# Row sums once per head pair in four column groups, one product for both heads in narrow slots, and a new spread of the shared bank

## The reference, cut to what matters

```python
q_blhd = jnp.einsum('bld,dhk->blhk', x_bld, Wq)
latent_bll = jnp.einsum('bld,dc->blc', x_bld, Wkv_down)
k_blhd = jnp.einsum('blc,chk->blhk', latent_bll, Wk_up)
v_blhd = jnp.einsum('blc,chk->blhk', latent_bll, Wv_up)
attn = jnp.einsum('bqhd,bkhd->bhqk', q_blhd, k_blhd) / 8
attn = softmax(where(key <= query, attn, -inf))
y_blhd = jnp.einsum('bhqk,bkhd->bqhd', attn, v_blhd)
x = layernorm(x + jnp.einsum('bqhd,hdo->bqo', y_blhd, Wout))
# then: router, top-1 expert with 320 places, gated expert, x + out * gate, layernorm
```

## Time and profile before

| | us |
|---|---|
| median of 3 runs | 2690.92 (2690.39 to 2691.18) |
| the profiled execution | 2683.09 |
| its span | 2681.3 |
| pairs of attention, from the first slot (51.4) to the last one's start (2319.6) | 2268.2 |
| PE busy | 2494.3 |
| POOL busy | 1701.7 |
| DVE busy | 1550.2 |
| ACT busy | 1002.2 |

### The profile page before, as it was taken

One profiled execution on the slowest core, in us unless ns is written; L12 is line 12 of the kernel. 1 busy time (PEld: TensorE's weight loads), 2 busy tenths in 40 slices (PEclk: granted clock), 3 DMA queues, 4 the chain that ended last, 5 costly groups with the idle time before them and its releaser, 6 DMA issues.

```text
span 2681.3 us, 35897 instructions
## 1 busy us (share of the span) xinstructions
PE 2494.3 (93%) x12072; PEld 1588.2 (59%) x12072; DVE 1550.2 (58%) x4378; ACT 1002.2 (37%) x1496; POOL 1701.7 (63%) x1671
## 2 busy tenths in 40 slices
PE   6999999999999999999999999999999999869996
PEld 4555665556655665566556655566556655646663
DVE  4566556665666566655665566656665665235553
ACT  3344334442444334433444244424443344112222
POOL 1677656865687658766786568656876578414444
PEclk7999999999999999999999999999999999879998
DMA  2121100200020001100110002000200011135441
GB/s 81 56 80 56 37 13 13 68 17 13 17 63 18 13 13 41 43 13 17 27 53 17 9 17 67 17 13 17 60 21 13 13 40 43 44 105 161 153 155 57
DMA packets 97062, 118.91 MB, mean 44 GB/s; under 512 B 12480, under 2 KB 75976, under 8 KB 96880
## 3 DMA queue, kind: packets, MB, share of 16 engines
q1 hardware_dynamic: 89712, 99.98, 13.3%
q0 software_dynamic: 7168, 16.64, 1.7%
HBM read 46.91 MB, written 37.90 MB: 32 GB/s over the span
## 4 chain that ended last, share of the span: by engine, by line
PE 63%; POOL 17%; issue 11%; DVE 5%; ACT 2%; DMA 0%; POOLq 0%; SPq 0%; ACTq 0%; DVEq 0%
PE value_ps L683 14%; POOL sums L464 10%; PE turned_ps L660 8%; PE row_ps L636 7%; PE turned_ps L663 7%; PE misc_ps L584 6%; PE turned_ps L844 5%; PE misc_ps L702 4%; PE misc_ps L693 4%; POOL probs L440 2%; PE value_ps L857 2%; PE misc_ps L857 2%; ACT probs L904 1%; POOL slots_x L497 1%; DVE masked_row L1056 1%
## 5 line engine op out<-in xcount | busy, mean ns | idle before, releaser
L904 ACT ACTIVATE probs<-turned_ps 128x1024 f32<-128x1024 f32 (+3 forms) x768 | 616.8, 811 | 959.6 <-PE turned_ps L663 951.3
L464 POOL TENSOR_TENSOR sums<-sums,probs 128x1024 f32<-128x1024 f32 (+3 forms) x512 | 830.2, 1622 | 23.2 <-ACT probs L904 14.2
L1056 DVE CUSTOM_DVE_ANT_0 masked_row<-row_ps,future 128x384 bf16<-128x384 f32 (+3 forms) x1024 | 464.2, 488 | 407.4 <-PE row_ps L636 406.2
L683 PE MATMUL value_ps<-probs,lat_keys 128*64 128x512 f32 (+3 forms) x3072 | 607.2, 507 | 44.7 <-POOL probs L440 41.3
L660 PE MATMUL turned_ps<-q_hl,lat_hi 128*128 128x512 f32 (+3 forms) x1536 | 569.6, 379 | 1.5 <-ACT fold_v L950 1.5
L663 PE MATMUL turned_ps<-q_max,lat_lo 65*128 65x512 f32 (+3 forms) x1536 | 528.0, 352 | 2.6 <-DMA q_max<-max_rows 2.6
L440 POOL TENSOR_SCALAR_AFFINE_SELECT probs<-probs 128x256 f32<-128x256 f32 x512 | 209.9, 410 | 498.1 <-ACT probs L904 497.4
L636 PE MATMUL row_ps<-lat_hi,q_hl 128*128 128x512 f32 (+3 forms) x1536 | 451.2, 365 | 14.2 <-DVE unit_max L1056 7.6
L460 POOL TENSOR_TENSOR sums<-probs 128x768 f32<-128x768 f32 (+1 forms) x128 | 268.6, 2098 | 229.9 <-ACT probs L904 229.9
L660 PEld LDWEIGHTS turned_ps<-q_hl,lat_hi 128*128 128x128 f32 x1536 | 293.8, 191 | 196.2 <-issue 148.3
L683 PEld LDWEIGHTS value_ps<-probs,lat_keys 128*64 128x64 f32 x3072 | 180.8, 137 | 348.8 <-issue 219.6
(11 more groups left out here) (183 smaller groups left out, 2408.7 us busy)
## 6 DMA issues: line engine op xcount, KB each, us to landing
q_max<-q_hl SPq DMA_DIRECT2D x256, 128.0 KB
slots_x<-zero_rows SPq DMA_DIRECT2D x8, 1290.0 KB, 6.2
ex_x<-slots_x SPq DMA_DIRECT2D x64, 129.0 KB, 3.5
x_in<-in_L_attn_x_bld SPq DMA_DIRECT2D x8, 1024.0 KB, 6.4
layer_out<-x_in SPq DMA_DIRECT2D x8, 1024.0 KB, 4.8
ex_w<-in_L_ffn_w_gate SPq DMA_DIRECT2D x32, 256.0 KB, 2.8
ex_w<-in_L_ffn_w_up SPq DMA_DIRECT2D x32, 256.0 KB, 3.2
ex_w<-in_L_ffn_w_down SPq DMA_DIRECT2D x32, 256.0 KB, 3.8
```

The source lines that it names most:

```text
L464: nc.gpsimd.tensor_tensor(sums[c][:, :, q0:BANK], sums[c][:, :, q0:BANK], now[:, :, q0:BANK], ALU.add).then_inc(added, 1)
L683: mm = nc.tensor.matmul(value_ps[h * LD:(h + 1) * LD, q0:BANK], lat_keys[b % 2][:, j, :], probs[:, n % NPROBS, h, q0:BANK], start=(j == 0) ...
L904: nc.scalar.activation(probs[:, n % NPROBS, :, q0:BANK], turned_ps[n % 2][:, :, q0:BANK], ACT.Exp).then_inc(exp_done, 1)
L1056: nc.vector.tensor_tensor_reduce(masked_row[n % 2][:, 0:width], row_ps[n % 2][:, 0:width], future[:, BANK - width:], scale=-1.0, scalar=-M ...
```

## The change

1. `total` runs once per pair, in slot 4 of the next pair, for both halves: four products with a weight of 32 columns of ones, each into its own 32 partitions (head 0 half 0, head 0 half 1, head 1 half 0, head 1 half 1). The sums of half 0 get two buffers.
2. `invert` is one transpose a pair. `invert_rows` takes the reciprocal twice, copies four blocks of 32 x 16 to the neighbouring partitions, and transposes both halves back, all in slot 5.
3. `divide` of the pair before moves on POOL from slots 0 and 6 to slots 6 and 10.
4. In slots with at most 256 queries (2, 3, 10, 11) both heads share one bank, and one product makes the scores of both.
5. The uses of the shared bank are spread anew (`maxT` of the next pair from slot 4 to 6, `proj`, `x1T`, `logits`, `pos` later), with `roots`, `variance`, `normalise` and `gate_exponentials`.
6. `wkv2`, `zero_rows` and the row maxima share memory with other tiles; `choose` waits once for the zero rows to be written.

```diff
-        sums = [sb(f"sums{c}", [P, 2, BANK], F32, attn) for c in range(2)]
+        half_sums = [sb(f"half_sums{i}", [P, 2, BANK], F32, attn) for i in range(3)]
+        sums_of = lambda gp, c: half_sums[2 if c else gp % 2]
...
-                EARLY[gp, 4] = [("maxT", gp + 1, 0)]
+                EARLY[gp, 6] = [("maxT", gp + 1, 0)]
             if gp:
-                late[4].append(("sums", gp - 1, 1))
-            late[6].append(("sums", gp, 0))
+                late[4].append(("sums", gp - 1))
...
             if b and p == 0:
-                for i, t in enumerate((3, 5, 7, 10, 11)):
+                for i, t in enumerate((9, 10, 11)):
                     late[t].append(("proj", b - 1, i))
             if b and p == 1:
-                for i, t in enumerate((3, 5, 7)):
-                    late[t].append(("proj", b - 1, 5 + i))
-                for kd in range(KD):
-                    late[10 + kd].append(("x1T", b - 1, 0, kd))
+                for i, t in enumerate((3, 5, 7, 9, 11)):
+                    late[t].append(("proj", b - 1, 3 + i))
             if b and p == 2:
-                for kd in range(KD):
-                    late[3 + 2 * kd].append(("x1T", b - 1, 1, kd))
-                late[7].append(("logits", b - 1))
+                for use, t in zip([(hf, kd) for hf in range(2) for kd in range(KD)], (3, 5, 7, 10)):
+                    late[t].append(("x1T", b - 1, *use))
+                late[11].append(("logits", b - 1))
             if b and p == 3:
-                late[3].append(("pos", b - 1))
+                late[7].append(("pos", b - 1))
...
-        for t, i in zip((1, 2, 3, 5, 7, 8, 9, 10), range(NT)):
+        for t, i in zip((8, 9, 9, 10, 10, 11, 11, 11), range(NT)):
             LATE[PAIRS - 1, t].append(("proj", LAST, i))
...
+        in_one_bank = lambda t: 2 * (BANK - first_query(t)) <= BANK
+        def scores_of(n):
+            q0 = first_query(n % NSLOT)
+            if in_one_bank(n % NSLOT):
+                return turned_ps[n % 2][:, 0, 0:2 * (BANK - q0)].rearrange("p (h q) -> p h q", h=2)
+            return turned_ps[n % 2][:, :, q0:BANK]
...
-                    if gp and t == 0:
-                        divide(gp - 1, 0)
-                    if gp and t == 6:
-                        divide(gp - 1, 1)
-                    if b and (p, t) in ((1, 0), (2, 0)):
+                    if gp and t in (6, 7 if gp == PAIRS - 1 else 10):
+                        divide(gp - 1, t // 7)
+                    if b and (p, t) in ((1, 8), (2, 2)):
                         roots(b - 1, p - 1)
...
+                if in_one_bank(t):
+                    nc.tensor.matmul(scores_of(n), lat_hi[b % 2][:, keys], q_hl[gp % 2][:, :, cols], start=True, stop=False)
+                    nc.tensor.matmul(scores_of(n), lat_lo[b % 2][:, keys], q_max[:, c, :, q0:BANK], start=False, stop=True
+                                     ).then_inc(turned_full, 1)
+                    return
...
-                    mm = nc.tensor.matmul(bank[h * LD:(h + 1) * LD, :], ones_f[:, :], sums[c][:, h, :], start=True, stop=True)
+                    for c in range(2):
+                        k = 2 * h + c
+                        mm = nc.tensor.matmul(bank[k * 32:(k + 1) * 32, :], ones_f[:, :], sums_of(gp, c)[:, h, :],
+                                              start=True, stop=True)
...
+                for c in range(2):
+                    nc.vector.reciprocal(rinv[:, c, :], cols).then_inc(inverse_done, 1)
+                dve.wait_ge(inverse_done, 6 * gp + 2)
+                for c in range(2):
+                    for h in range(2):
+                        src, dst = (64 * h + 32 * k for k in (c, 1 - c))
+                        nc.vector.tensor_copy(rinv[dst:dst + 32, c, :], rinv[src:src + 32, c, :]).then_inc(inverse_done, 1)
+                for c in range(2):
+                    dve.wait_ge(inverse_done, 6 * gp + 4 + 2 * c)
...
-                    if b and (p, t) in ((0, 11), (1, 8)):
-                        variance(b - 1, p)
-                    if b and (p, t) in ((1, 3), (2, 2)):
+                    if b and (p, t) in ((1, 5), (2, 0)):
+                        variance(b - 1, p - 1)
+                    if b and (p, t) in ((1, 10), (2, 4)):
                         normalise(b - 1, p - 1)
```

More of the change, by code:

```diff
@@ L132, in build_layer @@
         wr = sb("wr", [P, KD, E], F32, attn)
-        logit = sb("logit", [P, NT, E], F32, attn)
-        work_a = sb("work_a", [P, NT, E], F32, attn)
+        router = sb("router", [P, 2, NT, E], F32, attn)
+        logit, work_a = router[:, 0], router[:, 1]
+        zero_rows = router.rearrange("p k t e -> p (k t e)")[:, 0:W].rearrange("p (r w) -> p r w", r=1)
         work_b = sb("work_b", [P, NT, E], F32, attn)
@@ L240, in build_layer @@
         EARLY, LATE = {}, {}
+        last_sums = ("sums", PAIRS - 1)
         for gp in range(PAIRS):
@@ L276, in build_layer @@
         LAST = B - 1
-        for t, i in zip((1, 2, 3, 5, 7, 8, 9, 10), range(NT)):
+        for t, i in zip((8, 9, 9, 10, 10, 11, 11, 11), range(NT)):
             LATE[PAIRS - 1, t].append(("proj", LAST, i))
-        ENDING = ([("sums", PAIRS - 1, 1)] + [("rest", LAST, i) for i in range(NT)]
+        ENDING = ([last_sums] + [("rest", LAST, i) for i in range(NT)]
                   + [("x1T", LAST, hf, kd) for hf in range(2) for kd in range(KD)] + [("logits", LAST), ("pos", LAST)])
@@ L452, in add_probs @@
                 if c == 0 and j == 0:
-                    if gp:
-                        pool.wait_ge(misc_full, MISC["sums", gp - 1, 0] + 1)
-                    nc.gpsimd.tensor_copy(sums[0][:, :, 0:P], now[:, :, 0:P]).then_inc(added, 1)
+                    if gp >= 2:
+                        pool.wait_ge(misc_full, MISC["sums", gp - 2] + 1)
+                    nc.gpsimd.tensor_copy(sums_of(gp, 0)[:, :, 0:P], now[:, :, 0:P]).then_inc(added, 1)
                 elif j == 1:
                     if c == 1 and gp:
-                        pool.wait_ge(misc_full, MISC["sums", gp - 1, 1] + 1)
+                        pool.wait_ge(misc_full, MISC["sums", gp - 1] + 1)
                     before = probs[:, (n - 1) % NPROBS]
-                    nc.gpsimd.tensor_tensor(sums[c][:, :, q0:BANK], before[:, :, q0:BANK], now[:, :, q0:BANK], ALU.add
+                    nc.gpsimd.tensor_tensor(sums_of(gp, c)[:, :, q0:BANK], before[:, :, q0:BANK], now[:, :, q0:BANK], ALU.add
                                             ).then_inc(added, 1)
@@ L463, in add_probs @@
                     pool.wait_ge(added, gp * NADD + ADDS_OF[t] - 1)
-                    nc.gpsimd.tensor_tensor(sums[c][:, :, q0:BANK], sums[c][:, :, q0:BANK], now[:, :, q0:BANK], ALU.add
-                                            ).then_inc(added, 1)
+                    total = sums_of(gp, c)[:, :, q0:BANK]
+                    nc.gpsimd.tensor_tensor(total, total, now[:, :, q0:BANK], ALU.add).then_inc(added, 1)
             def divide(gp, c):
@@ L965, in _ @@
                         pass_alone(b - 1, t)
-                    if b and (p, t) == (2, 10):
+                    if b and (p, t) == (3, 4):
                         gate_exponentials(b - 1)
@@ L1071, in copy_max, with invert, invert_rows @@
                 nc.vector.tensor_copy(max_rows[c][:, :], bank[0:NT, 0:P]).then_inc(misc_free, 1)
-            def invert(gp, c):
-                use = ("sums", gp, c)
+            def invert(gp):
+                use = ("sums", gp)
                 bank = wait_full(dve, use)
                 nc.vector.transpose(sums_cols[:, :], bank).then_inc(free_of(use), 1)
-            def invert_rows(gp, c):
-                use = ("sums", gp, c)
-                n = 2 * gp + c
-                wait_emptied(dve, use)
-                nc.vector.reciprocal(rinv[:, :], sums_cols[:, :].rearrange("p (n q) -> p n q", q=32)[:, :, 0]
-                                     ).then_inc(inverse_done, 1)
-                dve.wait_ge(inverse_done, n + 1)
-                if gp:
-                    dve.wait_ge(normalised, n - 1)
-                nc.vector.transpose(rinv_rows[c][:, :], rinv[:, :].unsqueeze(2).to_broadcast([P, BANK // 32, 32])
-                                    ).then_inc(inverse_rows, 1)
+            def invert_rows(gp):
+                wait_emptied(dve, ("sums", gp))
+                cols = sums_cols[:, :].rearrange("p (n q) -> p n q", q=32)[:, :, 0]
+                for c in range(2):
[7 more added lines that the diff above has]
+                    dve.wait_ge(inverse_done, 6 * gp + 4 + 2 * c)
+                    if gp:
+                        dve.wait_ge(normalised, 2 * gp + c - 1)
+                    nc.vector.transpose(rinv_rows[c][:, :], rinv[:, c, :].unsqueeze(2).to_broadcast([P, BANK // 32, 32])
+                                        ).then_inc(inverse_rows, 1)
             def statistics(b, i):
@@ L1142, in choose @@
                 use = ("logits", b)
+                if b == 0:
+                    dve.wait_ge(zeroed, 16 * NPAIR)
```

19 lines of the change are left out of this document (9 added, 10 removed).

## The result

The changed kernel takes 2878.68 us (median of 4 runs, 2874.31 to 2880.65) against 2690.65 for the kernel before, run beside it. The ratio is 1.070, with a 95% interval of 1.068 to 1.072. It is slower by 188 us where I forecast 51 less. Its profiled execution has a span of 2875.0 and a mean granted clock of 0.938; before they were 2681.3 and 0.972.

What follows compares the result with a forecast made beforehand. PE, busy 93% of the span, was taken as the bound. Terms of -50, -11, -13, +12, -3, +14 and 0 gave -51 from 2690.9, so 2640 us; own range 2615 to 2668, 8-in-10 range 2600 to 2682.

Steps and rivals of the forecast that it cites:

- 0.44 for the copies: DVE's new block in slot 5: the four copies take 0.44 us, with 0.37 to 1.1 as bounds.
- Covered by 0.3: Slot 6's maxima end 0.3 us before PE needs them in slot 7; copies at 1.1 would cost 0.35 a pair.
- Rival E: DVE's block is late in each slot 7 by 0.35 to 0.8: +20 to +50, 2660 to 2690; chance 0.12.
- waits of 2.1 and 1.8: Pairs 6 and 7: PE's `maxT` waits this long for the bank, read out behind DVE's block; 7 pairs each.
- Total -7.2 each: Pairs 0 to 2 of sequences 1 to 7 together save 7.2 us per sequence, -50 over seven.
- 0.35 a wait: Average clock cost of a longer PE wait, from two of 14 earlier waits that cost 1.7 and 3.3.
- +14: Clock term of the sum: 41 more waits of 1.7 to 2.1 in the pairs add 14 us.
- Rival A: Each of 55 waits drops PE's clock for 3.4 us and costs 1.7: 2715, slower; chance 0.10.
- B: Sums' call: only two column groups run at a time, +54 us: 2694, no change; chance 0.10.
- C: Sums' call: program order forces five rounds, 2.25 a call, +80 us: 2720, slower; chance 0.05.
- 1.28 forecast: The division moved to slot 10 delays slot 11's select on POOL, so a plain pair ends 1.28 us later.
- D: The moved division costs nothing because POOL's chain behind slot 9 is shorter: 2586; chance 0.13.

Runs made afterwards that it cites:

- version of 2650.9: Changed kernel with reciprocals for the four copies and shared-bank uses moved, POOL's second division left in slot 10: 2650.9 us, ratio 0.987 to the kernel before.
- Experiment 8: Changed kernel plus five unused 512-column products on PE in slot 7 of each pair, behind its scores: 2898.3 us.

## Why the prediction was wrong

**The step that failed first** is the sentence on DVE: "0.44 for the copies (not in the trace; 0.37 to 1.1, by the reciprocal's 0.25 each)", and with it "Covered by 0.3". The copies took 2.7 a pair (4 x 0.668), beyond my upper bound, because I priced them from other small operations and left out that POOL can hold them. I had the cover about right: with four reciprocals, 1.07, slot 7 is only 0.12 longer than before, where I gave 0.35 for that case. The trace of before held the warning, a group that I didn't read:

```profile
L1128 DVE TENSOR_SCALAR var_eps<-mean_var x16: 169/170/2034, 356.9 to 2334.2; 128x4 f32<-128x4 f32 x16
```

Four elements a partition, a median of 0.17 and a longest of 2.03; seven of the sixteen take as long, and all seven start within an addition of POOL. Rival E had the right place, but 0.35 to 0.8 of lateness where 1.9 came.

**The shared bank.** For p 6 and 7 I forecast waits of 2.1 and 1.8; they were 4.1 and 3.8, and with reciprocals they are 2.4 and 2.0, so the copies made 1.8 of each. The wait for the queries at slot 9 of p 0 and 1 wasn't in my sum at all. I followed each use by its own work and not the bank from `q` at 8 to `proj` at 9, and so "Total -7.2 each" became +6 (measured from 125.7): p 0 to 2 hold 131.8 instead of the forecast 118.7. In the version of 2650.9, which keeps the division where I priced it, they hold 121.4; only with the division moved too is it 118.6. The terms that I wrote for p 0 to 2 also add up to 6.7 and not to 7.2.

**The clock.** "0.35 a wait" and "+14" came out as a clock loss of 103 more. I counted as new only the selects' waits and those of p 6 and 7; the ones of 1.15 in slot 7 and 2.4 in slot 9 came on top. For the selects' waits alone the rate wasn't far off: in the version of 2650.9, which has them nearly by themselves, the clock loss is 23 over that of before. My error was to take the 12 of 14 harmless waits of before as a rate for all kinds. After, a fall began in slot 7 or 8 behind the copies' wait in all 21 pairs p 3 to 5 of sequences 1 to 7. Experiment 8 shows that this wait causes the fall that comes right behind it. It does not show that the number of falls follows from the number of waits, since other falls came in their place. Rival A had this at 0.10 and 2715.

**What was right.** Four column groups run side by side: 0.99 for the call, against 0.95 forecast; B and C are out. Slot 3 is 0.20 shorter (0.22 forecast). The division costs 1.24 in slot 0 (1.28 forecast), and D is out. In plain pairs the wait ahead of `maxT` is gone. The wait behind the roots in slot 4 of p 2 is 1.67 (1.65 forecast). Slot 11 is 1.00, not 0.80: its scores are shorter by 0.15, and PE then waits as long for its row scores' bank. The version of 2650.9 is the change with the held copies and the conflicts on the bank taken out and the division left in, and my 2640 is 11 below it. That this is so near is partly luck: that version has no long waits in p 6 and 7, for which my sum holds +12, while p 0 to 2 give back 4.3 each and not 7.2, and p 3 gives 0.5 and not 1.6.

**The sum of the loss.** Undone alone, the copies give back 153, the bank's places 103, the division 37; undone together, 272. The 84 between 2606.8 and 2690.7 is what the change brings without them. 100 of the 272 are clock loss (178 to 78), the rest waiting. How the clock's part divides among the three stays open, since each alone gives back 50, 59 and 8, more together than the 100.

## What to carry to other kernels

Before a small operation on DVE is priced by its size, look in the trace for the spread (shortest, median, longest) of operations of its kind that run beside POOL. Here a longest of twelve times the median was the sign that POOL can hold them, and whether it did hung on the form of the instruction and the moment of its start. Follow a shared buffer from user to user, with the read-out that frees it, and not each user apart. A forecast that adds waits to the engine that is the bound should carry the clock as a case of its own, for each new wait that recurs in every round.

## What the runs showed that I had not expected

A reciprocal of 0.245 us runs beside POOL where a copy of 0.17 waits 2.27. Transposes, reductions and reciprocals on DVE never grew beside POOL's additions (a transpose back takes 0.67 to 0.72 in all traces); copies (0.17 to 2.32), scalings (0.41 to 1.55) and two-input operations from SBUF (0.17 to 2.33) did.

Four products in four column groups take the time of one: the call's eight instructions start in two rounds of four, the four of a round within 0.02 us and the second round 0.45 behind the first. The group's row of the kernel after, by form, mean 0.612 for one instruction of which four lie side by side:

```profile
L709 PE MATMUL misc_ps<-half_sums,ones_f 128*32 128x512 f32 x504 | 68.0, 612 | 0.0
```

The call before had four instructions in two groups and took 0.95; this one has eight in four and takes 0.99, where one behind the other they would be eight times 0.43 to 0.5. Estimated so, it is 3.5 to 4 times as fast. The Trainium skill (TensorE: Matmul & The Clock Gate, Part 3: Packing small matmuls) gives 2.38 for three column tiles and has no figure for four of them alone; here four give 3.5 or more, by that estimate. Whether its rule of starts strictly in program order is broken can't be read from the records, which don't say which product an instruction belongs to, so my "the trace disagrees with it" said too much; the price that I worked out from the rule for this call, 2.25, didn't come.
